# Merged convolution projections, a group norm and output projection split by channel halves, and two ones-sums fewer on GpSimd, in a conv/attention/FFN block

## The reference

```python
# 1. channel attention: c = 32
q = conv1x1(x, Wq, bq); k = conv1x1(x, Wk, bk).reshape(N, c); v = conv1x1(x, Wv, bv)
x = conv1x1(softmax(q @ k) @ v, Wo, bo) * gamma + x
# 2. differential attention over the 1024 tokens, 8 heads of 32, then group norm (4 groups of 64 channels)
t = tokens(x); a = layernorm(t)
o = (softmax(q1 k1) - lam * softmax(q2 k2)) @ v         # per head
y = groupnorm(o.T) * gn_w + gn_b
t = t + y.T @ out_w.T + out_b
# 3. shared expert and 8 routed experts, top 2 of 8
t = t + ffn(layernorm(t))
```

## Time and profile before

| | |
|---|---|
| Median of 3 runs | 6759.91 us (6759.73 to 6770.47) |
| The profiled execution's own time | 6765.27 us |
| Its span, first to last instruction | 6763.5 us |
| PE busy | 6217.3 us (92%) |
| DVE busy | 4643.0 us (69%) |
| ACT busy / POOL busy | 3065.6 us (45%) / 3140.7 us (46%) |
| One image | 418.2 us, from the first group sum (355.6) to the last (6629.3) over 15 |

### The profile page before, as it was taken

One profiled execution on the slowest core, in us unless ns is written; L12 is line 12 of the kernel. 1 busy time (PEld: TensorE's weight loads), 2 busy tenths in 40 slices (PEclk: granted clock), 3 DMA queues, 4 the chain that ended last, 5 costly groups with the idle time before them and its releaser, 6 DMA issues.

```text
span 6763.5 us, 126375 instructions
## 1 busy us (share of the span) xinstructions
PE 6217.3 (92%) x41746; PEld 4006.5 (59%) x41746; DVE 4643.0 (69%) x6438; ACT 3065.6 (45%) x5422; POOL 3140.7 (46%) x1414
## 2 busy tenths in 40 slices
PE   7989899898999989999999999999999899998998
PEld 4565565655656556565665656556565565655656
DVE  5757677676776767767677675776757667576675
ACT  3535445254452544535345353453534535354353
POOL 3706437074370734707347172461725617255271
PEclk9999999899998999999999999999999999999999
DMA  2202121121221212202021120211202112021120
GB/s 74 48 23 53 31 46 44 29 51 25 46 44 29 52 29 45 49 22 56 24 48 45 27 57 18 49 45 28 56 18 53 41 32 57 13 54 40 36 53 16
DMA packets 111103, 271.61 MB, mean 40 GB/s; under 512 B 33872, under 2 KB 56528, under 8 KB 101968
## 3 DMA queue, kind: packets, MB, share of 16 engines
q1 hardware_dynamic: 110416, 262.72, 16.8%
HBM read 23.38 MB, written 16.78 MB: 6 GB/s over the span
## 4 chain that ended last, share of the span: by engine, by line
PE 82%; DVE 7%; issue 5%; ACT 2%; POOL 2%; DMA 1%; SPq 0%; DVEq 0%; ACTq 0%; POOLq 0%
PE psum L802 19%; PE psum L977 17%; PE psum L935 14%; PE psum L916 13%; PE psum L1026 5%; PE psum L942 4%; DVE minus_max L590 2%; PE psum L820 2%; POOL prob_sums L314 2%; PE psum L956 1%; PE psum L865 1%; PE psum L1055 1%; PE psum L827 1%; PE psum L891 1%; DVE max_rows L599 1%
## 5 line engine op out<-in xcount | busy, mean ns | idle before, releaser
L314 POOL TENSOR_TENSOR prob_sums<-probs 128x1024 f32<-128x1024 f32 x768 | 1831.6, 2385 | 3333.3 <-ACT probs L399 3047.3
L399 ACT ACTIVATE probs<-psum 128x512 f32<-128x512 f32 x4096 | 2223.4, 595 | 1423.9 <-PE psum L977 1412.3
L590 DVE TENSOR_REDUCE minus_max<-psum 128x1 f32<-128x1024 f32 x2048 | 2422.6, 1209 | 405.1 <-PE psum L916 397.7
L977 PE MATMUL psum<-stack 98*128 98x512 f32 x4096 | 1483.9, 439 | 43.8 <-ACT probs L399 41.7
L916 PE MATMUL psum<-stack 96*128 96x512 f32 x4096 | 1244.4, 413 | 105.1 <-DVE max_rows L600 64.8
L314 POOL TENSOR_TENSOR prob_sums<-prob_sums,probs 128x1024 f32<-128x1024 f32 x512 | 1220.2, 2383 | 101.8 <-ACT probs L399 62.9
L977 PEld LDWEIGHTS psum<-stack 98*128 98x128 f32 x4096 | 706.9, 191 | 737.3 <-ACT probs L399 478.5
L935 PE MATMUL psum<-probs,v_tokens 128*32 128x256 f32 x16384 | 1107.1, 388 | 0.0
L916 PEld LDWEIGHTS psum<-stack 96*128 96x128 f32 x4096 | 725.8, 192 | 406.1 <-DVE max_rows L600 170.9
L802 PE MATMUL psum<-act_hi,w_hi 128*128 128x512 f32 x1856 | 781.3, 421 | 130.8 <-DVE act_lo L697 72.9
L802 PE MATMUL psum<-act_hi,w_lo 128*128 128x512 f32 x1856 | 757.8, 408 | 0.0
(11 more groups left out here) (133 smaller groups left out, 4593.8 us busy)
## 6 DMA issues: line engine op xcount, KB each, us to landing
stack<-stage SPq DMA_DIRECT2D x1024, 128.0 KB, 3.0
stack<-stage SPq DMA_DIRECT2D x256, 256.0 KB, 3.1
x_tile<-x_dram SPq DMA_DIRECT2D x17, 1024.0 KB, 4.9
x_tile<-o_head SPq DMA_DIRECT2D x512, 32.0 KB, 1.9
stack<-max_rows SPq DMA_DIRECT2D x512, 4.0 KB
y_dram<-residual SPq DMA_DIRECT2D x16, 512.0 KB, 2.8
y_dram<-stage SPq DMA_DIRECT2D x16, 512.0 KB, 3.7
stage<-w_split_dram SPq DMA_DIRECT2D x1, 3848.0 KB, 12.7
```

The source lines that it names most:

```text
L314: nc.gpsimd.tensor_tensor(total, first, probs[:, k % NP, :], ALU.add).then_inc(sum_pool, 1)
L399: nc.scalar.activation(probs[:, k % NP, half * HALF:(half + 1) * HALF], ps[:, 4 + half, :], ACT.Exp).then_inc(p_ready, 1)
L590: v.tensor_reduce(nm[:, u % 2, q:q + 1], flat_in, AX.X, ALU.max, negate=True).then_inc(ring_free, 1)
L977: mm(ps[:, 4 + half, :], stack[0:KS, s, 1, kt * P:(kt + 1) * P], stack[0:KS, s, 0, half * HALF:(half + 1) * HALF], start=True, stop=True). ...
```

## The change

1. **Convolution.** q, v and k of x come from one product per half (96 rows out instead of 64, weights `wqvk[:, kt, :]`), both halves right behind `tokens`. The separate q product is gone; q is brought to its transposed form by 8 transposes of `qvk_sb[0:32]`, read with a stride of 8, in FFN step 9 (bank 7). ACT takes both halves out of PSUM behind the layer norm. The biases come as one column by two small strided loads at the start.
2. **Group norm by channel halves.** Half 0 holds heads 0 to 3, half 1 heads 4 to 7. Sums of half 0 are made in unit 15; its variance, root and coefficients stand ahead of the last head's reciprocals on DVE; ACT then writes the full and the high parts of half 0. Half 1 follows the last head. The root takes the epsilon as its bias, so an addition goes.
3. **Output projection** goes over channel half 0 for all four results first, then over half 1 (3 matmuls each).
4. **Last unit.** Tiles 6 and 7 of unit 15 are summed by ones-matmuls of their own (`alone`); POOL adds only (0, 1, 2) and (3, 4, 5). DVE, not POOL, adds the two softmaxes of the last head.
5. In `statistics` two independent operations stand ahead of a waiting one.

```diff
+def sum_groups(u):
+    return ((0, 1, 2), (3, 4, 5), (6, 7)) if u < UNITS - 1 else ((0, 1, 2), (3, 4, 5))
+def alone(u):
+    return () if u < UNITS - 1 else (6, 7)
...
-    return k if i else (k + 2) % 4
+    return (0, 1, 4, 5)[k] if i else (k + 2) % 4
...
             sp.dma_start(wf[:, :], w_full).then_inc(full_in, 16)
+            sp.dma_start(bqvk[0:CR], w_full[0:1, F_VEC + V_BQ:F_VEC + V_BQ + CR].rearrange("o c -> c o"), allow_slow_non_contiguous=True).then_inc(full_in, 16)
+            sp.dma_start(bqvk[CR:3 * CR], w_full[0:2 * CR, F_VEC + V_BVK:F_VEC + V_BVK + 1],
+                         allow_slow_non_contiguous=True).then_inc(full_in, 16)
...
-                add_head(HEADS - 1)
...
+                norm_coefficients(0)
+                for s in range(2):
+                    act.wait_ge(o_in[s], (b * (HEADS // 2) + HEADS // 4) * 4 * 16)
+                for half in range(NH):
+                    norm_heads(0, half, on_sb)
+                    norm_heads(0, half, xh).then_inc(on_hi, 1)
+                norm_coefficients(1)
                 for s in range(2):
                     act.wait_ge(o_in[s], (b + 1) * (HEADS // 2) * 4 * 16)
                 for half in range(NH):
+                    norm_heads(1, half, xh).then_inc(on_hi, 1)
                 normalise(b, 1)
                 layer_norm(1)
+                for half in range(NH):
+                    conv_vk(b + 1, half)
...
+                norm_variance(0)
+                norm_rest(0)
+                for part in range(RECIPS):
+                    sum_recips(UNITS - 1, part)
+                head_out(UNITS - 1)
+                dve.wait_ge(o_free, (b + 1) * UNITS)
+                v.tensor_tensor(oh[:, (HEADS - 1) % 2, :], oh[:, (HEADS - 1) % 2, :], ot[:, :],
+                                ALU.add).then_inc(oh_ready, 1)
                 head_statistics(HEADS - 1)
+                norm_sums(1)
+                norm_low(0, 0)
+                norm_variance(1)
+                norm_rest(1)
+                norm_low(0, 1)
...
             def conv_q(n):
-                pe.wait_ge(x_in, n * 16 + 16)
-                xq = xin[:, :, :].rearrange("p t (m r) -> p t r m", r=NR)
+                qr = qvk_sb[0:CR, :].rearrange("p (m r) -> p r m", r=NR)
                 for r in range(NR):
-                    for kt in range(CT):
-                        last = mm(ps[:, 1, r * CR:(r + 1) * CR], xq[:, kt, r, :], wqvk[:, kt, 0:CR],
-                                  start=(kt == 0), stop=(kt == CT - 1))
+                    last = nc.tensor.transpose(ps[:, 7, r * CR:(r + 1) * CR], qr[:, r, :],
+                                               wf[0:CR, F_ID:F_ID + CR])
...
                         tokens(b, 1)
-                    if i == 1:
-                        conv_q(b + 1)
-                        conv_vk(0)
+                        for half in range(NH):
+                            pe.wait_ge(y1_ready, b * 4 + 4)
+                            conv_vk(b + 1, half)
...
-                for k in range(4):
-                    half = k // 2
-                    pe.wait_ge(on_lo, b * NH * CT + CT * half + CT)
-                    split_mm(ps[:, k, :], W_O + (k % 2) * P, (C, P),
-                             slice(half * HALF, (half + 1) * HALF)).then_inc(y1_full, 1)
+                norm_groups(1)
+                for kt in range(CT):
+                    for k in range(4):
+                        half = k // 2
+                        pe.wait_ge(on_lo, b * NH * CT + NH * kt + half + 1)
+                        for n, (wt, xx) in enumerate(((wh, xh), (wl, xh), (wh, xl))):
+                            w = W_O + kt * C + (k % 2) * P
+                            last = mm(ps[:, k, :], wt[:, w:w + P], xx[:, kt, half * HALF:(half + 1) * HALF],
+                                      start=(kt == 0 and n == 0), stop=(kt == CT - 1 and n == 2))
...
+                    if i == NE:
+                        conv_q(b + 1)
...
-                        conv_vk(1)
                         pe.wait_ge(cb_lo, b + 1)
```

More of the change, by code:

```diff
@@ L60, in adds @@
     u, kt = divmod(tile, NT)
-    upto = max([kt] + [group[1] for group in SUM_GROUPS if kt == group[0]])
-    return len(ADDED_KT) * u + sum(at <= upto for at in ADDED_KT)
+    upto = max([kt] + [group[1] for group in sum_groups(u) if kt == group[0]])
+    return sum(at <= u * NT + upto for at in ADDED)
 def ones_after(u, pair):
@@ L300, in _ @@
                 for u in range(UNITS):
-                    for g, group in enumerate(SUM_GROUPS):
+                    for g, group in enumerate(sum_groups(u)):
                         n = u * GROUPS + g
@@ L645, in _ @@
                     ring_step(item)
-                for u in range(UNITS + 1):
+                for u in range(UNITS):
                     for pair in range(PAIRS):
@@ L846, in conv_last @@
                 mm(ps[:, 2 + k, :], a2_sb[:, (k % 2) * P:(k % 2 + 1) * P],
-                   vk_sb[0:CR, (k // 2) * HALF:(k // 2 + 1) * HALF], start=True, stop=True).then_inc(c_full, 1)
+                   qvk_sb[CR:2 * CR, (k // 2) * HALF:(k // 2 + 1) * HALF], start=True, stop=True).then_inc(c_full, 1)
+            for half in range(NH):
+                conv_vk(0, half)
+            pe.wait_ge(vk_ready, NH)
             conv_q(0)
-            for half in range(NH):
-                conv_vk(half)
             conv_scores(0)
```

183 lines of the change are left out of this document (97 added, 86 removed).

## The result

The changed kernel takes 6538.8 us (median of 4 runs, 6533.5 to 6542.1) against 6759.8 for the kernel before, run beside it on the same chip (4 runs, 6758.1 to 6770.5). The ratio is 0.9669, 95% interval 0.9652 to 0.9686: 221 us less. The direction was right, and two fifths of the gain were not foreseen. The profiled execution took 6536.0, its span is 6533.1 (before: 6763.5).

A forecast was written before the change was run, and what follows sets the result against it. PE, busy 92% of the span, was taken as the bound. 5.6 + 6.1 + 0.2 - 1.9 - 2.0 = 8.0 us an image, 128 in 16, with 6 at the start 134: 6759.9 becomes 6626 us, range 6585 to 6690.

The forecast's parts named there:

- Group norm and projection: From the last head's reciprocals through the output projection: PE starts projecting 5.9 us earlier, additions end 0.3 later; 5.6 us gained per image.
- Convolution: Between token transposes and those back: merged products take 3.9 us, the layer norm ends later, at 5.05; 6.1 us gained per image.
- Start: From the first products to the first scores, once per execution: 17.1 us become some 11, 6 gained.
- q transposes: Eight new strided transposes on PE in FFN step 9, 0.24 us each: 1.9 us lost per image, between 1.0 and 3.8.
- Clock: PE idling ahead of the transposes back and of step 1's last matmul lowers its clock: 2.0 us lost per image, bounds 0 and 5.
- convolution with the statistics: The convolution's gain of 6.1 us per image, plus 0.2 saved by the statistics of the other layer norm.
- The clock holds: Rival, chance 0.10: PE keeps 2.4 GHz ahead of the projection and at the two later places; 12.2 us an image, 6560.
- The clock falls further: Rival, chance 0.15: merged products at half clock, 4 us lost at the router and behind; 3.9 us an image, 6692.
- slower than before: Rival, chance 0.04: PE at half clock from the transposes back into the experts; with 24 us of it, about 6783.
- The gain is waited away: Rival, chance 0.02: PE waits for the new x before the transposes back; landing 15 us after issue gives about 6757.

The follow-up runs named there:

- e1_conv_only: Kernel before with only the convolution's part of the change (merged products, q transposes in step 9, biases); old group norm, projection and sums kept: 6663.1 us, ratio 0.9849.
- f1_fill_router: Changed kernel with 8 matmuls of unused result put in front of PE's wait for DVE's routing table: 6515.0 us, ratio 0.9630 to the kernel before.
- e2_norm_only: Changed kernel with the old convolution put back; split group norm and projection, ones-sums and reordered statistics stay: 6639.5 us, ratio 0.9805 to the kernel before.
- f2_fill_gap: Changed kernel with 16 matmuls of unused result ahead of the last head's group sum, where PE idles before the projection: 6523.3 us, ratio 0.9645 to the kernel before.

## Why the prediction missed

**Group norm and projection: right.** 5.6 us were forecast, A and B give 6.11 (6.20 - 0.09). From the start of the last reciprocals to the projection 4.57 us were measured (4.7 forecast), and PE's idle time ahead of the group sum was 4.31 (5). The group sum of half 0 costs less than I put down for it: 0.2 us in the stream of unit 15 (from its start to that of the next product, mean of 16 images), not 0.4. The projection kept its length, at the half clock for 5.4 us of it, as assumed. PE didn't starve between the two halves.

**Convolution: right.** 6.1 forecast, C gives 5.97. The merged products ran at the full clock in 3.60, and the layer norm was the later one. `e1_conv_only` has 5.72 of it by itself.

**Start: right.** 6 forecast, 6.6 measured.

**q transposes: oversized.** The step "8 x 0.24 = 1.9 us" failed: they take 1.06, and 0.11 each when more follow. The pace of 0.22 to 0.24 was that of loads of 128 rows with their matmuls in the earlier trace rows; I took it for the price of the stride. The stride is the same here, and the pace is that of unstrided transposes. Those q products also differed in being full float32 products and not transposes; which of the two, that or the 128 rows, made them slow, no run here shows. I had gone by the row against the price in the Trainium skill (TensorE: Matmul & The Clock Gate, LDWEIGHTS), which made 0.9 of the eight; the measurement is nearer to that estimate. The lower bound, 1.0, was the right value.

**Clock: wrong in place and in sign.** The step "I take **2.0 us lost** for both places, nearer to the router's" failed. At the router nothing was lost: D became 0.73 shorter, since before it had 1.8 us at half clock and after it has none. Behind the routing-table wait the loss was there, 0.84 by `f1_fill_router`, and it needed no long wait of its own (2.35 us). In sum, D and the clock's share of E, +0.1 instead of +2.0. The reasoning was that idle time where products ran before must cost clock. It treats each place by itself, and the router does not behave so. D has 1.8 us at half clock before, 2.8 with the convolution's half alone (`e1_conv_only`), 1.5 with the other half alone (`e2_norm_only`), and none with both. `f2_fill_gap` shows how far such a coupling reaches: filling the gap ahead of the projection brought the fall at the router, in 9 of 15 images, that I had forecast for the kernel after. What decides whether the clock falls at a place stays open.

**The end of the image: not looked at.** F and G give 3.36 us an image, about 50 us in 15 images, and had no term. This is the largest part of the miss: a term that the sum put at nothing without a reason. 2.55 of it goes with the second stop behind the loop's jump (1.7 the stop itself, the rest less half clock), gone because the code ahead of the loop is shorter by 24 matmuls. The chain's 5% of issue in the earlier trace rows was passed over; the waits of PE by line had shown 30 stops for 16 images, at a line that nobody edits. The remaining 0.81 in G lies in several small stretches and moves with half clock; I can't tie it to an instruction.

By terms, in us an image and forecast against measured: group norm and projection 5.6, 6.1; convolution with the statistics 6.3, 6.0; q transposes -1.9, -1.1; clock at the router and behind it -2.0, -0.1 (D's 0.73 less the 0.84); end of image and elsewhere 0, 3.4. The small rest of E, 0.14, is left. The first three make 10.0 and 11.0, and the miss is mainly the last two. That the total lay only 46 us outside the range says nothing for the two terms that failed.

**The rivals.** "The clock holds" did not come in its own place (the projection stayed at half clock), so its time of 6560 came near by luck, for other reasons. `f2_fill_gap` is what it described for the projection, and shows why its sum would not have held: B does end with 6.58, and D pays for it. "The clock falls further" and "slower than before" have nothing for them in the kernel after. "The gain is waited away" did not come either: in the fourth image x landed ahead of its products in the kernel after, and made them wait only in the kernels with a filler (1.50 us in `f2_fill_gap`), where the layer norm hid it or nearly.

## What to carry to other kernels

Read the waits of a loop's first instructions, with their counts, before costing a change: a stop that comes twice a pass at a line with nothing to wait for can be a wait for instructions that hangs on where the loop's head lies in the program (see whether a packet of an instruction queue lands just ahead of its end), and some 20 matmuls ahead of the loop can give or take it (here 38 to 47 us of 6760). When a change shortens a kernel by removing waits, the clock of the places behind it moves too, in both directions, and a sum of places costed one by one can miss that; test it with idle-time matmuls, and try them in every wait of a stretch, since the fall can move to the next one (6515 and 6523 us with one filler, 6520 with both, 6495 with three). Price a small operation by its own shape where two rows differ in more than one thing: rows of 128, a full float32 product and a stride were one row here.

## What the runs showed of the hardware

- A stop of 1.85 us (fourth image of the kernel before) behind the tenth of 16 like matmuls just after a loop's jump, with no semaphore, that comes or goes with 20 to 24 matmuls ahead of the loop. A stop at the run's start comes in every kernel here; both come in three of them (59.0, 54.4 and 50.3 us in 30 stops, against 29.2 to 34.7 us in 15). All 240 stops in 13 traces end 1.2 to 1.8 us behind the landing of a 16 KB packet of the instruction queue 8.
- The same instructions with the same waits (0.70 and 1.32 us) ran the router at PEclk 1.00 in all 15 images of the kernel after, and fell to 0.50 in 9 of 15 with the gap ahead of the projection filled (D 16.84 without the fall, 18.4 with it). More work earlier can make a later place slower.
- Transposes of 32 rows, strided by 8 elements in their load, go at 0.11 to 0.13 us each, as fast as the unstrided 128-row ones (1.94 / 16 = 0.12, L939), though the load by itself is longer (medians 198 and 141 ns).
